# Experts of a routed feed-forward in 64-row chunks, stationary in column halves of the array

## What is computed

```python
raw_gate = softmax(x @ gate)                    # 16 experts
_, topk_idx = top_k(raw_gate, 3)
gate_topk = mask * raw_gate / sum(...)
hidden = relu(einsum('btd,edh->bteh', x, W1) + b1)      # 512 -> 1024
expert_out = einsum('bteh,ehd->bted', hidden, W2) + b2  # 1024 -> 512
return einsum('bte,bted->btd', gate_topk, expert_out)
```

## Time and profile before

| | before |
|---|---|
| three runs | 1173.19, 1174.76, 1182.06 us |
| median | 1174.76 us |
| the profiled execution's own time | 1176.1 us |
| its span, first to last instruction | 1174.2 us |
| TensorE busy | 1062.3 us (90%) |
| VectorE, ScalarE, GpSimd busy | 454.9, 349.0, 217.4 us |
| mean granted TensorE clock | 0.961 |

### The profile page before, as it was taken

The page is one execution under the profiler, slowest core; times in us unless marked ns, Lnnn a source line. Parts: engine busy times, 40 slices in busy tenths (PEclk is TensorE's granted clock), DMA queues, the critical chain, the costliest instruction groups (busy, mean ns, idle before and its releaser), DMA issues. The chain is left out here.

```text
span 1174.2 us, 17359 instructions
## 1 busy us (share of the span) xinstructions
PE 1062.3 (90%) x5421; PEld 691.1 (59%) x5422; DVE 454.9 (39%) x1694; ACT 349.0 (30%) x827; POOL 217.4 (19%) x340
## 2 busy tenths in 40 slices
PE   8966679955989999999999999899999989999997
PEld 7962235533467677767767777565456655555553
DVE  5837888884670000000000000047855643111212
ACT  3633765771122222222222222133254420000000
POOL 2763031110001111111111111100030001121211
PEclk9987899977988999999999999989999999999999
DMA  8767005117616755865595555560030004000000
GB/s 311 231 122 275 4 1 174 68 54 184 230 49 198 255 182 188 278 234 187 182 331 189 181 187 182 153 208 1 1 144 1 2 10 152 1 0 1 16 13 28
DMA packets 71802, 152.83 MB, mean 130 GB/s; under 512 B 12066, under 2 KB 16298, under 8 KB 70910
## 3 DMA queue, kind: packets, MB, share of 16 engines
q1 hardware_dynamic: 63494, 131.21, 32.4%
q0 software_dynamic: 6928, 17.04, 6.3%
q10 hardware_dynamic: 1320, 3.84, 1.4%
HBM read 131.83 MB, written 20.25 MB: 130 GB/s over the span
## 5 line engine op out<-in xcount | busy, mean ns | idle before, releaser
L1330 ACT ACTIVATE att<-ba,b 128x128 f32<-128x128 f32 x216 | 79.4, 368 | 308.2 <-PE ba L1300 308.2
L1350 DVE TENSOR_TENSOR att<-ba,att 128x512 f32<-128x512 f32 x27 | 18.7, 691 | 369.4 <-PE ba L1308 369.4
L1300 PEld LDWEIGHTS ba<-tiles,shared 128*128 128x128 f32 x896 | 111.5, 192 | 37.4 <-issue 37.4
L1300 PEld LDWEIGHTS ba<-tiles,Wmem 128*128 128x128 f32 x832 | 105.5, 195 | 38.9 <-issue 38.6
L1300 PE MATMUL ba<-tiles,shared 128*128 x896 | 114.4, 276 | 1.2 <-issue 0.6
L1300 PE MATMUL ba<-tiles,Wmem 128*128 x832 | 108.3, 279 | 5.5 <-issue 4.5
L1308 PE MATMUL ba<-shared,att 128*128 128x512 f32 x224 | 110.0, 593 | 0.0
L1308 PE MATMUL ba<-Wmem,att 128*128 128x512 f32 x208 | 102.3, 594 | 0.1
L2419 PE MATMUL acc<-tiles 128*128 128x400 f32 x256 | 90.6, 505 | 0.0
L2485 DVE SCALAR_TENSOR_TENSOR tiles<-bf,shared 128x400 f32<-128x400 f32 x64 | 32.4, 566 | 129.9 <-PE bf L2404 129.6
L2378 PE MATMUL bf<-shared,Wmem 128*128 128x400 f32 x192 | 71.2, 507 | 2.3 <-PEq L49 1.5
(11 more groups left out here) (396 smaller groups left out, 1673.9 us busy)
## 6 DMA issues: line engine op xcount, KB each, us to landing
Wmem<-in_W SPq DMA_DIRECT2D x16, 2048.0 KB, 14.2
shared<-in_W SPq DMA_DIRECT2D x16, 2048.0 KB, 13.2
cT<-in_ctxT SPq DMA_DIRECT2D x8, 1444.0 KB, 14.0
ctx_rows<-in_ctx SPq DMA_DIRECT2D x8, 1280.0 KB
Wmem<-in_Wkv SPq DMA_DIRECT2D x2, 2048.0 KB, 9.2
att<-in_b SPq DMA_DIRECT2D x16, 256.0 KB, 14.2
tiles<-in_WoT SPq DMA_DIRECT2D x4, 1024.0 KB
Wmem<-in_WiT SPq DMA_DIRECT2D x3, 1024.0 KB, 7.3
```

The lines of the kernel that those rows point to most:

```text
L1300: ins = pe.matmul(ph[j % NH][:, :], W1[u][:, k, j * P:(j + 1) * P], xgT[:, bass.ds(w, 1), k * P:(k + 1) * P].rearrange("p o t -> p (o t)") ...
L1330: act.activation(hT[:, j, :], ph[j % NH][:, :], ACT.Relu, bias=b1[:, bass.ds((e + u) * HJ + j, 1)]).then_inc(relu_ok, 1)
```

## The change

An expert's rows are now cut into chunks of Q = 64 rows (at least two for each expert), and the roles of the operands in the first layer are exchanged. The 64 rows are stationary, `xT[:, k, :]` of 128 x 64, and 512 columns of `W1` move. Half h = 0 of the hidden features goes to output partitions 0 to 63 and h = 1 to 64 to 127, that is to the two column halves of the array. The second layer does the same with 256 columns of `W2` for each half. A chunk's gathered rows lie in the same form, 128 half rows of 256 numbers (`half_rows`). Since the first layer now leaves rows on partitions, its sums (`pa`) are copied to `pre`, half by ScalarE and half by VectorE, and four transposes (`turn_hidden`) turn them before bias and ReLU, of which ScalarE and VectorE take four pieces each.

The order on TensorE, in `step(c)`: the four transposes of chunk c's hidden sums, two transposes of the rows of chunk c + 2 (counted as the gathers are), the whole first layer of chunk c + 1, the second layer of chunk c. The turned rows, the gathered rows and the first layer's sums each have one buffer. GpSimd copies the numbers of the target rows only when the output is there (`scatter`), has two output buffers, and waits for the landing of a scatter only where rows of two experts could meet. SyncE asks for `W1` of expert e + 2 already when the last first layer of expert e is done. The tables of `route` have 66 columns instead of 34.

```diff
+Q = P // 2
+DQ = D // 2
+CHUNKS = 66
-        KB, NT = TOPK * B, SLOT_TILES
+        KB, NT = TOPK * B, CHUNKS
-                indirect_dma_start(out=res["xg_sb"][:, i, :], in_=res["xn_d"], ...)
+                indirect_dma_start(out=res["xg_sb"][:, i, 0:DQ], in_=half_rows(res["xn_d"]), ...)
...
     def expert_sp(sp):
...
-                sp.wait_ge(py_rd, done + 1)
-                load(e + u, u)
+                sp.wait_ge(a_mm, done)
+                first(e + u, u)
+                sp.wait_ge(py_rd, done + 1)
+                second(e + u, u)
...
     def expert_pe(pe):
+        def first_layer(w):
             for k in range(KD):
+                for h in range(2):
+                    ins = pe.matmul(pa[h * Q:(h + 1) * Q, :], xT[:, k, :], w[:, k, h * HH:(h + 1) * HH], start=k == 0, stop=k == KD - 1)
+            ins.then_inc(a_mm, 1)
+
+        def turn_rows(src):
+            for m in range(2):
+                ins = pe.transpose(px[:, m * P:(m + 1) * P], src[:, m * P:(m + 1) * P], ident[:, :])
             ins.then_inc(xt_mm, 1)
+        def turn_hidden(c):
+            pe.wait_ge(a_rd[0], c)
+            pe.wait_ge(a_rd[1], c)
+            pe.wait_ge(h_ok[0], JH * c)
+            pe.wait_ge(h_ok[1], JH * c)
+            for i in range(2):
+                for n in range(2):
+                    q = 2 * i + n
+                    ins = pe.transpose(pt[i][:, n * P:(n + 1) * P], pre[:, q * P:(q + 1) * P], ident[:, :])
+                ins.then_inc(t_mm, 1)
+
+        def second_layer(c, w):
+            pe.wait_ge(py_rd, c)
+            for i, n, half, j in turned:
+                pe.wait_ge(h_ok[i], JH * c + 2 * n + half + 1)
+                for h in range(2):
+                    ins = pe.matmul(py[h * Q:(h + 1) * Q, :], hT[:, j, :], w[:, j, h * DQ:(h + 1) * DQ],
+                                    start=j == 0, stop=j == HJ - 1)
+            ins.then_inc(y_mm, 1)
+
+        def step(c, w1, w2):
+            turn_hidden(c)
+            pe.wait_ge(xg_in[1], 16 * c + 16)
+            pe.wait_ge(xt_ok, c + 1)
+            turn_rows(rows)
+            first_layer(w1)
+            second_layer(c, w2)
...
     def expert_act(act):
+        def keep_rows(c):
+            act.wait_ge(xt_mm, c + 2)
+            act.wait_ge(a_mm, c + 1)
+            act.copy(xT..., px...).then_inc(xt_ok, 1)
...
     def expert_dve(dve):
+        def output(c, u, y, y_out, before):
+            dve.wait_ge(y_mm, c)
+            dve.tensor_tensor(raw, py, b2[u], ALU.add).then_inc(py_rd, 1)
+            dve.wait_ge(py_rd, c + 1)
+            dve.wait_ge(y_out, before)
+            dve.tensor_scalar(y, raw, res["gate_s"][:, bass.ds(c - 1, 1)], None, ALU.mult).then_inc(y_ok, 1)
...
     def expert_pool(pool):
+        def gather(c):
+            pool.wait_ge(xt_mm, c + 2)
+            pool.tensor_copy(from_row[:, :], res["gidx"][:, bass.ds(c + 2, 1)]).then_inc(from_ok, 1)
+            pool.wait_ge(from_ok, c)
+            pool.indirect_dma_start(out=rows, in_=half_rows(res["xn_d"]), ...).then_inc(xg_in[1], 16)
+
+        def scatter(c, y, to_row, y_out):
+            pool.wait_ge(y_ok, c)
+            pool.tensor_copy(to_row[:, :], res["oidx"][:, bass.ds(c - 1, 1)]).then_inc(to_ok, 1)
+            pool.wait_ge(to_ok, c)
+            pool.indirect_dma_start(out=half_rows(res["sum_d"]), in_=y, compute_op=ALU.add, ...).then_inc(y_out, 16)
+                with pool.Fori(m0 + 1, m1 + 1) as m:
+                    gather(m + e + u)
+                    pool.wait_ge(last_out, 16 * e + 16 * u + 16)
+                    pool.wait_ge(more_out, 16 * m0 + 16)
+                    scatter(m + e + u, y_more, to_more, more_out)
+                gather(m1 + e + u + 1)
+                scatter(m1 + e + u + 1, y_last, to_last, last_out)
```

More of the change, by code:

```diff
@@ L1213, with half_rows @@
 NKD = C + S
+def half_rows(rows):
+    return rows.rearrange("r (h d) -> (r h) d", h=2)
 def expert_parts(io, res, sb, sem, bank):
@@ L1220, in expert_parts @@
     W2 = [res["W_second"], res["shared"][:, KD * H:2 * KD * H].rearrange("p (j d) -> p j d", d=D)]
+    HH, JH = H // 2, HJ // 2
     b1 = sb("b1", [P, E_N * HJ])
[L1222 to L1232, removed]
+    pieces, xg = res["att"], res["xg_sb"]
+    hT = pieces[:, 0, :].rearrange("p (j s) -> p j s", s=Q)
+    pre = pieces[:, 1, :]
+    raw, y_last, y_more = pieces[:, 2, 0:DQ], pieces[:, 2, DQ:D], pieces[:, 3, 0:DQ]
+    b2 = [pieces[:, 4, u * DQ:(u + 1) * DQ] for u in range(2)]
+    xT = pieces[:, 5, 0:KD * Q].rearrange("p (k s) -> p k s", s=Q)
+    first_rows, rows = xg[:, 0, 0:DQ], xg[:, 1, 0:DQ]
@@ L1257, in expert_sp @@
         bias(0, 0)
-        load(1, 1)
+        first(1, 1)
+        second(1, 1)
         sp.dma_start(res["vec"][:, :, :], io["vec"]).then_inc(res["vec_in"], 16)
@@ new lines, in step, with expert @@
+        def step(c, w1, w2):
[5 more added lines that the diff above has]
+            second_layer(c, w2)
+        pe.wait_ge(xg_in[0], 16)
+        turn_rows(first_rows)
+        pe.wait_ge(w1_in[0], 16)
+        pe.wait_ge(xt_ok, 1)
+        pe.wait_ge(xg_in[1], 16)
+        turn_rows(rows)
+        first_layer(W1[0])
+        def expert(e, u, base):
+            c0, c1 = chunks_of(pe, e)
+            pe.wait_ge(w2_in[u], 24 * base + 48)
+            with pe.Fori(c0 + 1, c1) as c:
+                step(c, W1[u], W2[u])
+            pe.wait_ge(w1_in[1 - u], 8 * base + 16 + 16 * u)
+            step(c1, W1[1 - u], W2[u])
@@ L1629, in _ @@
             full_pe(pe)
[L1630 to L1631 removed]
+            pe.wait_ge(last_out, 16 * E_N + 16)
             keep_awake(pe, sum_b, ident, 25)
@@ L2526, in build @@
         res["xg_sb"] = sb("xg_sb", [P, NG, D])
+        res["gidx"], res["oidx"] = (res["xg_sb"][:, 2, i * NTB:(i + 1) * NTB].bitcast(I32) for i in range(2))
+        res["gate_s"] = res["xg_sb"][:, 2, 2 * NTB:3 * NTB]
         res["Wmem"] = sb("Wmem", [P, 2 * KD * H])
```

223 lines of the change are left out of this document (120 added, 103 removed).

## The result

The changed kernel took 1210.22 us in the median of four runs (1206.93 to 1216.67), the kernel before 1173.97 (1172.18 to 1182.06): a ratio of 1.032, with an interval of 1.0286 to 1.0353. The forecast was 1156, and the range ended at 1206. The profiled execution took 1213.48 us with a span of 1211.8, 37.4 us more than the 1176.1 of before.

What follows compares the result with a forecast made beforehand. TensorE's own work was taken to bound the kernel. Terms -69.2 + 17.8 + 13.5 - 1 + 13.5 + 0.5 + 5.6 = -19.3 took 1176.1 to 1156.8, 1155.5 against the median; forecast 1156 us, range 1142 to 1206.

Steps and rivals of the forecast that it cites:

- Streaming: Expert stage products: column halves run in full pairs, 6.88 us a chunk; the total goes from 378.8 to 309.6, -69.2 us.
- rivals 3 and 4: Column halves: 3, their loads stay exposed, 86 us, 1242, chance 0.07; 4, they don't run at once, about 1465, 0.08.
- Transposes, change of shape, handoffs: TensorE work between a chunk's layers: six transposes +17.8 us, array shape changes +13.5, handoffs -1.
- natural step: One chunk's step on TensorE: 6.88 + 0.66 + 0.30 + 0.20 = 8.04 us.
- The wait for rows: TensorE before the row transposes: a step can't be shorter than 4.1 us plus the gather's landing; +13.5 us (0 to 92).
- rival 1: GpSimd's queue sets the step: gathers land in 5.1 us, every step is 9.2, waits 52 us, 1194; chance 0.20.
- rival 2: Scatter order at expert boundaries: an expert's first chunk waits for the previous expert's last scatter; 27 us, 1183; chance 0.17.
- Start of the stage: First chunk's first layer has no cover, +3.44 us; start and end of the pipeline together +0.5 us.
- Routing: Routing before the experts: tables widen from 34 to 66 columns, all exposed, +5.6 us, from 4 to 8.

Runs made afterwards that it cites:

- four_warm: Changed kernel with four products that nobody reads put ahead of the wait for rows in every step; 1186.1 us, ratio 1.011.
- gather_first: Changed kernel with GpSimd gathering one chunk further ahead, each gather asked for before the scatter of the step before it; 1154.2 us, ratio 0.982.
- turn_late: Changed kernel with the row transposes moved between the two layers, so rows are needed 3.5 us later; 1150.6 us, ratio 0.979.
- w1_late: Changed kernel with W1 asked for together with W2 at the end of the expert; 1200.8 us, ratio 1.024.

## Why the prediction was wrong, step by step

**Streaming: right.** 6.88 us were predicted for a chunk and 7.04 measured (3.48 + 3.56). The halves run in full pairs, and rivals 3 and 4 are out. The Trainium skill, "TensorE: Matmul & The Clock Gate", Part 3, The mechanism, says in one sentence that a weight load overlaps only where row groups differ; its first paragraph also allows one into a background buffer. Here the measurement decides against the one sentence: a pair of loads of 64 columns takes 0.14 us, the next pair comes 0.43 later, and the products lose nothing by it, with 16 records in 3.48 us.

```profile
371.41 0.14 PEld L1318 LDWEIGHTS ba<-Wmem,att 128*64 128x64 f32 x2 [0.28 <-issue]
371.84 0.14 PEld L1318 LDWEIGHTS ba<-Wmem,att 128*64 128x64 f32 x2 [0.29 <-issue]
```

**Transposes, change of shape, handoffs: right in sum.** 1.16 us were predicted (0.66 + 0.30 + 0.20) and 0.80 measured. The natural step was to be 8.04 and is 7.84, which over 44 steps gives 9 us more than I had counted. The handoffs before, read from the stage that ended too early, were 0.43 us a tile and not 0.37.

**The wait for rows: here it failed.** The condition was right (a step cannot be shorter than 4.1 us plus the landing, and the stop is seen where that is over 7.84), the resource was right, and rival 1 named it. The term was mis-sized: 13.5 us, with 48.6 measured. I took the landing's median of before for most chunks. But before, a gather was asked for only when the scatter ahead of it had landed, 10.3 us after the scatter (523.60 and 533.86 in the earlier trace rows) and 11.0 after the second layer's weights (SyncE asked for them at 522.82 in the same trace), when their load was mostly through (it landed in 14.2). The changed kernel asks for it 1.05 us behind the end of the scatter's issue, with a load in full flight. So the row's median did not describe the new place of the instruction, and even its longest value, 6.0, was passed by ten gathers. My argument that W1 is asked for a step earlier was true and no help: 16 of the 18 late gathers stand behind an expert's last scatter or the first loads, and the early W1 hit two more by itself (391.16 and 480.35) and stood beside five of the 16. Rival 1's 52 us is close to the wait, although it had every chunk 1.2 us late, where 17 steps were 1.8 to 3.6 us late.

**The clock: missing.** No term of the sum and no rival had it. The stage before ran at 0.99 and had no stops of this kind, and I carried that level over to a stage for which I had myself predicted waits. 24.1 us in first layers are the second price of the stops, and four_warm bears them out. Up to 2.6 us in the row transposes may belong to it as well.

**Scatter order (rival 2): refuted** as the cause by gather_first. **Start of the stage:** the first chunk's first layer took 6.41 us where I had 3.44, at the lower clock (0.54 from 361.90 to 368.00). The kernel before began its stage at it too (0.50 from 355.90 to 360.00), so only part of this is a loss against it; I had missed it in both. **Routing:** +7.5 against +5.6, within the 4 to 8 given. The fills and the three gate products came as predicted (2.15 against 2.3; 5.25 against 5.5), and so did L1186 (1.80 against 1.94); what was low was the work around them: from L1186 to the gate products it grew by 3.5 us (8.65 to 12.16) where I had 2.6, and behind them by 1.6 (2.22 to 3.77) where I had 0.3.

Put together: the stage was to shrink by 24.9 us, to 375.8, and took 434.3. Of the 58.5 us between the two, waits make 35.1, the clock 24.1 and the row transposes 2.6, the pauses at experts' starts 2.2, less 8.8 for the shorter step: 55.2. The rest is mostly the first chunk's slow start. The terms of streaming, transposes and shape were right; the wait for rows was mis-sized, the clock behind it was missing, and the two decided.

## What to carry to other kernels

A DMA's landing time belongs to the place in the program from which it was asked for. Before such a row is used for a moved instruction, ask what is in flight at its new place, and take the longest value for every issue that falls beside a bulk load, and know that even this was passed here (6.0 in the rows before, 6.9 in the new place). When a predicted wait leaves TensorE idle for 2 to 3 us, add a second term for the clock, and look first for a place later in the step where the wait costs nothing: two lines moved were worth 60 us here, as much as a different prefetch order (56) within the spread of the runs, and more than any delay of the loads.

## What the runs showed of the hardware

- **Gather beside a bulk load.** An indirect gather landed in 2.8 us (the median with small loads) and in 5.4 to 6.9 beside a load of 2 MB. It mattered when the load was asked for: 4.3 to 4.4 us before the gather gave 5.4 to 6.0, at the same moment or 0.3 us before 6.6 to 6.9, and 0.8 us or more behind it 2.7 to 3.4 (changed kernel). Two loads, both 3.7 to 4.2 us before, gave 6.2 to 6.7 (w1_late).
- **The clock behind a stop.** After 13 of the 17 stops, a first layer of 3.48 us took 4.67 to 6.25, which costs up to 2.8 us. At the lower of the two levels (1.2 GHz) the whole layer took 6.41: its pairs start every 0.85 us and not every 0.43, as these loads between them show (timeline of the changed kernel, start of the stage):

```profile
362.81 0.24 PEld L1318 LDWEIGHTS ba<-Wmem,att 128*64 128x64 f32 x2 [0.62 <-issue]
363.66 0.24 PEld L1318 LDWEIGHTS ba<-Wmem,att 128*64 128x64 f32 x2 [0.62 <-issue]
```

  Not every stop has this effect: behind the 2.56 us at 529.57 the clock stayed at 1.00, and behind the 3.15 us at 508.14 it fell. What decides between the two stays open; no run here tried for it.
- **Column halves of f32 products** share the time fully, 16 records of 512 columns in 3.48 us.
- **A change of array shape** and back costs 0.3 us (8.14 against 7.84 in turn_late).
